# One partial sum of a fused GNN and FFN kernel moved from VectorE to ScalarE and GpSimd in five work units

## The reference

```
x = x + gnn(layernorm(x), src, dst)          # 20000 edges: mean of neighbours, two 512x512 products, leaky relu, row norm
x = x + ffn(layernorm(x))
def ffn(x):                                   # w_gate, w_up: 1408 x 512; w_down: 512 x 1408
    gate = x @ q(w_gate).T;  up = x @ q(w_up).T
    return (silu(gate) * up) @ q(w_down).T
def q(w):                                     # per row and group of 128 inputs
    scale = mean(abs(group)) + 1e-5
    return clip(round(group / scale), -1, 1) * scale
```

## Time and profile before

| | |
|---|---|
| median of three runs | 363.95 us |
| profiled execution, device time | 365.24 us |
| its span, first to last instruction | 363.3 us |
| TensorE busy with matmuls | 329.8 us (91% of the span) |
| VectorE busy | 304.6 us (84%) |
| ScalarE busy | 238.0 us (66%) |
| GpSimd busy | 163.1 us (45%) |
| mean granted clock of TensorE | 0.987 of full |

### The profile page before, as it was taken

The page is one execution under the profiler, slowest core; times in us unless marked ns, Lnnn a source line. Parts: engine busy times, 40 slices in busy tenths (PEclk is TensorE's granted clock), DMA queues, the critical chain, the costliest instruction groups (busy, mean ns, idle before and its releaser), DMA issues.

```text
span 363.3 us, 5834 instructions
## 1 busy us (share of the span) xinstructions
PE 329.8 (91%) x1623; PEld 249.6 (69%) x1623; DVE 304.6 (84%) x789; ACT 238.0 (66%) x637; POOL 163.1 (45%) x223
## 2 busy tenths in 40 slices
PE   1997879899999999999687999999999999999992
PEld 0443335554545578777476898989899898889991
DVE  3569999899889248999696998999999989999994
ACT  2155958899787136774656768668777678676670
POOL 7000000110010590110003466888788787799992
PEclk9999999999999999999988999999999999999998
DMA  7961322233232001200000000000000000000215
GB/s 226 291 159 33 86 58 78 68 88 87 59 82 79 3 3 35 74 22 2 0 1 2 0 3 0 3 0 0 2 3 2 0 0 3 0 3 0 73 44 169
DMA packets 9412, 16.69 MB, mean 46 GB/s; under 512 B 1062, under 2 KB 1886, under 8 KB 9378
## 3 DMA queue, kind: packets, MB, share of 16 engines
q1 hardware_dynamic: 9300, 16.21, 15.9%
q10 hardware_dynamic: 78, 0.08, 0.1%
HBM read 13.73 MB, written 2.56 MB: 45 GB/s over the span
## 4 chain that ended last, share of the span: by engine, by line
PE 58%; DVE 26%; ACT 10%; issue 3%; POOL 1%; DVEq 0%; ACTq 0%; POOLq 0%
PE bank L1320 39%; PE bank L1208 7%; PE bank L1250 5%; DVE tq_gu L901 4%; DVE hot_dst L1005 3%; ACT mag_early L690 3%; DVE tq_d L901 2%; DVE hot_src L996 2%; ACT a_t L742 2%; DVE bn L1061 2%; ACT hot_src L675 2%; DVE x_sb L1058 2%; DVE z L1040 1%; PE bank L1232 1%; PE bank L1156 1%
## 5 line engine op out<-in xcount | busy, mean ns | idle before, releaser
L1320 PE MATMUL bank<-x_hi,t_gu 128*128 128x378 f32 (+1 forms) x264 | 96.9, 367 | 3.6 <-DVE x_lo L1075 2.8
L1320 PE MATMUL bank<-x_lo,t_gu 128*128 128x378 f32 (+1 forms) x264 | 95.5, 362 | 0.0
L1208 PE MATMUL bank<-w_sb,xnT 128*125 128x512 f32 x160 | 86.9, 632 | 4.8 <-ACT z L725 4.1
L1114 DVE SCALAR_TENSOR_TENSOR g_acc<-bank,nscale,g_acc 128x378 f32<-128x378 f32 (+1 forms) x99 | 64.3, 650 | 12.1 <-PE bank L1320 10.8
L612 POOL TENSOR_SCALAR thr<-absum 128x4 f32<-128x4 f32 (+1 forms) x34 | 10.7, 315 | 121.5 <-ACT mag_early L690 97.2
L1114 DVE SCALAR_TENSOR_TENSOR u_acc<-bank,nscale,u_acc 128x378 f32<-128x378 f32 (+1 forms) x99 | 64.1, 647 | 0.0
L633 POOL TENSOR_TENSOR acc<-acc,d_one 128x378 f32<-128x378 f32 (+1 forms) x58 | 60.9, 1052 | 0.1
L643 POOL TENSOR_TENSOR hh<-sg,u_acc 128x378 f32<-128x378 f32 (+1 forms) x32 | 35.1, 1098 | 57.4 <-ACT sg L830 57.3
L1320 PEld LDWEIGHTS bank<-x_hi,t_gu 128*128 128x128 f32 x264 | 51.1, 193 | 8.1 <-DVE x_lo L1075 3.5
L1320 PEld LDWEIGHTS bank<-x_lo,t_gu 128*128 128x128 f32 x264 | 51.0, 193 | 3.6
L1167 PEld LDWEIGHTS bank<-hot_dst,hot_src 128*125 128x125 bf16 x157 | 20.8, 137 | 42.0 <-DVE hot_dst L1005 23.0
(11 more groups left out here) (136 smaller groups left out, 558.5 us busy)
## 6 DMA issues: line engine op xcount, KB each, us to landing
raw<-in_L_ffn_w_gate SPq DMA_DIRECT2D x11, 256.0 KB, 2.7
raw<-in_L_ffn_w_up SPq DMA_DIRECT2D x11, 256.0 KB, 2.6
out_x<-x_sb SPq DMA_DIRECT2D x10, 224.0 KB
raw<-in_L_ffn_w_down SPq DMA_DIRECT2D x8, 256.0 KB, 2.7
x_sb<-in_x SPq DMA_DIRECT2D x1, 1344.0 KB
w_sb<-in_L_gnn_W_neigh SPq DMA_DIRECT2D x1, 1024.0 KB, 6.0
w_sb<-in_L_gnn_W_self SPq DMA_DIRECT2D x1, 1024.0 KB, 7.3
raw<-in_L_ffn_w_down SPq DMA_DIRECT2D x4, 192.0 KB, 2.3
```

The costliest lines, as they stand in the source:

```text
L1114: nc.vector.scalar_tensor_tensor(out=to, in0=bank_of(u, what)[:, 0:w], scalar=nscale[:, j:j + 1], in1=to, op0=ALU.mult, op1=ALU.add).then_ ...
L1208: last = nc.tensor.matmul(to[0:TP, :], xnT[:, t, k * TP:(k + 1) * TP], w_sb[:, k, half * D:(half + 1) * D], start=k == 0, stop=k == KD - 1)
L1320: last = nc.tensor.matmul(to, w, parts[h], start=h == 0, stop=h == 1)
```

## The change

For units 0 to 4 the second up piece U1 is taken by ScalarE with its scaled copy into a slot of `d_one` (slots that D1 uses from unit 2 on), and GpSimd adds it onto `u_acc`. VectorE no longer touches U1 in these units, and its U2 waits for GpSimd's addition. In ScalarE's order the new take stands behind silu(n-1) and D1(n-3), ahead of `h_hi(n-1)`; in step 0, where neither exists, it stands behind `normalize1(8)` and `x1_high(7)`. In GpSimd's order the new addition stands behind `hh(n-1)` and the addition of D1(n-3), ahead of `h_lo(n-1)`. TensorE's order is the same; the bank of U1 is now released by ScalarE.

```diff
+        EARLY = 5
...
-            return what in ("G0", "U0") or what in ("D1", "D3")[:2 if u < NU - 1 else 0]
+            return what in ("G0", "U0") or what == "U1" and u < EARLY or what in ("D1", "D3")[:2 if u < NU - 1 else 0]
...
-            if by_act(*p) and (p[1] == "O" or p[1][0] == "D" and UNITS[p[0]][0]):
+            if by_act(*p) and (p[1] in ("O", "U1") or p[1][0] == "D" and UNITS[p[0]][0]):
...
-            o = {"D1": 0, "D3": 1}[p[1]] if p[1] != "O" else len([q for q in stage if q[1] == "O"]) % 2
+            o = {"D1": 0, "D3": 1, "U1": 0}[p[1]] if p[1] != "O" else len([q for q in stage if q[1] == "O"]) % 2
...
                     add_down(n - LAG, "D1")
+                if (n, "U1") in added:
+                    o, slot = stage[n, "U1"]
+                    pool.wait_ge(act_took, took[n, "U1"])
+                    to = u_acc[:, n % 2, 0:width(n)]
+                    nc.gpsimd.tensor_tensor(to, to, d_one[:, o, slot, 0:width(n)], ALU.add).then_inc(d_added, 1)
...
+                    if what == "D1" and n < NU and by_act(n, "U1"):
+                        o, slot = stage[n, "U1"]
+                        if (n, "U1") in slot_before:
+                            act.wait_ge(d_added, added[slot_before[n, "U1"]])
+                        take(n, "U1", d_one[:, o, slot, 0:width(n)])
...
                 if what in ("G1", "U1"):
                     dve.wait_ge(act_took, took[u, what[0] + "0"])
+                elif what == "U2" and (u, "U1") in added:
+                    dve.wait_ge(d_added, added[u, "U1"])
```

## The result

The changed kernel takes 368.67 us (median of four, 368.02 to 371.94), the kernel before 364.07 us in the same comparison: a ratio of 1.0126, 95% interval 1.0097 to 1.0155. It is 1.3% slower. The profiled execution took 368.82 us with a span of 366.9 us, against 365.24 and 363.3 before.

A forecast was written before the change was run, and what follows sets the result against it. Bound: a chain of waiting instructions up to X9, then saturated PE. 4.14 us for unit 0 plus 0.85 for the clock, 0 elsewhere, gave 5.0 on 363.95: 368.9 us, own range 366.9 to 369.8 (chance 0.80).

The forecast's parts named there:

- The bound: PE saturated from X9 at 198.5 us, before it a chain of waiting instructions; any delay of X9 moves all behind it.
- Unit 0, the place of the take: In unit 0, ACT's take of U1(0) queues behind `x1_high(7)` and its wait for X7, delaying U2(0) through POOL.
- The size of the first link: In unit 0, U2(0) on DVE starts 4.34 us later and nrm, first instruction of `residual(9)`, 4.14 us later.
- What is queued behind it: On DVE behind U2(0): G3(0), U3(0), `residual(9)`, `x1_low(7)`; they pass the delay on, no slack found before X9.
- Units 1 and 2: U2 waits for POOL there, but slack covers it: sum 0; without cover up to 2.05 us and 0.9 us.
- Units 3 and 4, SP, the ring: U2 waits some 0.4 us for POOL, G1(1) 0.4 us for U1(0)'s bank, SP gets nothing new: sum 0.
- The clock term: PE's clock may fall to half rate behind X9: between 0 and 1.7 us, middle 0.85 us taken.
- the low stretch before X9: Second clock fall of PE in the kernel before, said to cost nothing since PE waited for X9 anyhow.
- X7 at full rate: In unit 0, X7 without the low clock comes about 1.2 us earlier, making the price 2.95 us instead of 4.14.
- The sum: Whole kernel: 4.14 + 0.85 = 5.0 us slower, added to the median 363.95 gives 368.9 us.

The follow-up runs named there:

- `units1to4`: Changed kernel's edit for U1 of units 1 to 4 only, U1(0) left with DVE: 364.77 us beside 365.07 for the kernel before, ratio 0.9996.
- `take_first`: Changed kernel, but in step 0 ACT takes U1(0) ahead of normalizing tile 8 and the wait for X7: 365.03 us, ratio 1.001.
- `norm_between`: Changed kernel with ACT's normalizing of tile 8 moved behind the high part of tile 7, ahead of the take: 370.22 us, ratio 1.0154.
- `late_add`: Changed kernel, but DVE's U2 waits for U0 alone and POOL adds U1 behind DVE's U3: 364.87 us beside 364.64, ratio 1.0009.
- `resid_look_a`: Profiled execution of the changed kernel with DVE's statistics of tile 9 moved behind G2(0), inside its wait for POOL: 364.63 us.
- `unit0_only`: Changed kernel's edit for U1 of unit 0 only, units 1 to 4 as in the kernel before: 368.93 us, ratio 1.0125.
- `before_resid_early`: Kernel before, with DVE's statistics of tile 9 ahead of G1(0) and ACT's root ahead of the X7 wait: 364.21 us, ratio 0.9994.
- `after_look_a`: The changed kernel, unaltered, profiled once more for its spread: 367.45 us.

## Why the prediction was right, point by point

- **The bound.** Right. PE saturates at X9, does the same work behind it in the same time (151.40 against 151.48 us), and nothing is caught up. The relief of DVE was worth nothing (`units1to4`).
- **Unit 0, the place of the take.** Right, and shown from both sides: ahead of the wait the price is 0.5 us (`take_first`), behind it 4.0, behind one instruction more a further 0.70 at U2(0) (`norm_between`). The price passes through DVE's wait for POOL alone (`late_add`).
- **The size of the first link.** Forecast 4.34 us at U2(0) and 4.14 at nrm. Measured from the first FFN matmul: 188.23 - 177.59 = 10.64 against 184.16 - 178.03 = 6.13, so 4.51, and 12.21 against 7.89, so 4.32. The step on ACT from the high part of tile 7 to the take was 0.49, not 0.57. That was more than made up by two others: the high part itself started 0.20 us later against the first matmul (8.40 against 8.20), as X7 did by 0.27, since the low clock began earlier against the FFN's start, and from POOL's start to U2(0) it was 1.10 us, not 1.03.
- **What is queued behind it.** Right: from nrm to X8 it is 192.74 - 185.92 = 6.82 us before and 196.62 - 189.80 = 6.82 after. I named two carriers, the statistics and the low part of tile 7. Both are: the statistics end last in the changed kernel, and with them out of the way the low part and its T block are the chain (`resid_look_a`). What I did not say is how close behind the second path is.
- **Units 1 and 2.** Right: waits of 1.98 and 1.90 us for POOL in `units1to4`, no price.
- **Units 3 and 4, SP, the ring.** Nothing seen there, as forecast; PE waits 0.44 us for the bank of U1(0), inside the stall.
- **The clock term.** This one failed. I put 0.85 us, the middle of 0 and 1.7, on a fall of the clock behind X9. In none of the five profiles of the changed kernel and of `unit0_only`, and in none of the other kernels, is the clock low in the 150 us behind X9; PE's idle time there was 1.5 us, not 2.2. The rule that the forecast took from the Trainium skill ("TensorE: Matmul & The Clock Gate", section "What's actually happening": the slow rate is the default, recent activity lifts it) agrees with the traces in direction, since every low stretch in the FFN's start came behind idle time of PE; taken strictly, for a fall behind X9 for certain, it said too much: no fall came behind the 1.5 us of idle time ahead of X9, nor behind the 2.05 to 2.24 us ahead of X8 in `units1to4`, `take_first`, `late_add` and `before_resid_early`, where 2.05 us in the kernel before was followed by one. And the low stretch before X9, which I had called free, was not: at half rate PE made ACT's take of G0(2) and U0(2) wait, and X8 to X9 took 5.78 us, against 5.48 in the changed kernel, where this work ran at full rate. The term was -0.30 where I had +0.85.
- **X7 at full rate.** The lower end of the forecast's range took 1.2 us off the price for this, and no row of the prediction gives that number. In `after_look_a` X7 ran at full rate (0.59 us), but the low stretch then lay ahead of it, and the wait on ACT ended at 8.14 us behind the first matmul instead of 8.40: 0.26 us, and X9 at 24.25 instead of 24.51. No profile has X7 sooner than 7.05 us behind the first matmul, so the 1.2 us were seen in none.
- **The sum.** 4.32 - 0.30 = 4.02 us between first matmul and X9, where the forecast had 4.14 + 0.85 = 5.0. The medians of the first comparison are 4.6 us apart (368.67 and 364.07, four executions each); the 0.6 us above 4.02 is no part of the mechanism that I can show. That 368.9 still stands beside 368.67 is in part chance: I added 5.0 to a median of 363.95 from three executions, and later comparisons put the kernel before at 365.07 (23 executions) and 364.64 (29 executions). Against the first of them the changed kernel is 3.4 us slower by the medians and 1.0101 by the ratio.

## What to carry to other kernels

When work moves to an idle engine, ask what the new instruction is queued behind on that engine, not how idle it is: ACT was idle for 3 us with the operand ready, and the take still came last because the wait in front of it belonged to other work. The same wait for a helper engine cost 4 us in one unit and nothing in the next two; what decides is which instructions are queued behind the one that waits, and whether one of them starts a chain. Where an accumulation order ties a fast engine to a slow one, adding the late term last can loosen it: here that took the whole price away (`late_add`), though it gained nothing on the kernel before.

## What the runs showed of the hardware that I had not expected

One kernel's executions fell into two groups 2.4 us apart (364.6 to 365.0 and 367.1 to 367.4). In the profile of the upper group PE ran the FFN's second unit at 0.50 of its clock, in those of the lower group at full rate, with the same 2.46 us of idle time ahead of it in all three. The same idle time, then, may or may not be followed by the slow level, so a price for it cannot be read from one trace. PE at half rate cost 2.1 us there, where the work between T block and X9 was on the chain, and 0.3 us in the kernel before, where most of it was not.
